# Token-major norms and gated output weights in a kernel with two interleaved batches

## The chip, the cores and the metric

The kernel runs on one core of a Trainium2 chip. The metric is device time in microseconds for one launch. Of the kernel before three runs are shown; their median counts.

## The reference, cut to what matters

Sixteen batches of 512 tokens with 128 channels pass through an adaptive layer: a norm with a scale and shift per batch, an attention with 16 heads, a gated addition to x, a second such norm, and a two-layer windowed transformer with a gated addition.

```python
mod = (_silu(c) @ wmod).reshape(16, 6, 1, -1)
sa, ca, ga, sb, cb, gb = (mod[:, i] for i in range(6))
ga, gb = ...                                # magnitude at least 0.25
h = _layernorm(x) * (1 + ca) + sa
x = x + ga * attn(h)                        # causal, 16 heads of 8, output @ W_O
h = _layernorm(x) * (1 + cb) + sb
x = x + gb * ffn(h)                         # 2 layers: windowed attention, norm, gated GELU
```

## The kernel before

All 16 batches are independent; batch b uses buffer set b % 2, and two batches are always in work: while one is in its attention (`max`, `score`, `ctx`, `turn`), the other is in the transformer (`qkv`, `rotate`, `wscore`, `wexp`, `share`, `pturn`, `wctx`, `wout`, `hid`, `down`). Every batch is one list of some 190 steps (`steps()`, line 55). A step is named, and each engine has its own code for it (`step` in each engine's function); the engines meet through semaphores, and PSUM banks are handed out in the order of a written table (`Banks.take`, line 202), whose waits stand on TensorE.

The order is written by hand tables. `PLACES` (line 91) is one order of the steps for all engines, `PARTS` says which engines take part, and `TURNS` (line 114) merges the two running batches on each engine. `merged` (line 136) joins them.

Activations lie channels in the partitions, tokens along the free dimension. The first norm (n = 0) goes so: `load` transposes x on TensorE (4 transposes of 128x128), ScalarE copies the result into `xT1` (line 664), GpSimd keeps a copy `xT` (line 1013); `center` multiplies with the centring matrix (line 444, one float32 product 512 wide, two instructions); ScalarE squares (676); `spread` multiplies with the averaging matrix (458); ScalarE takes Ln and Exp (685, 687); VectorE multiplies with the scale (865) into `y1`; the shift enters later as `added`, its products with the three weights, in lines 696, 875 and 731. From `y1` come queries, keys (470) and values (474). Their three bfloat16 parts are spread over partitions by DMAs (line 1080).

The attention ends with `join` (transposes, line 731), `out` (544: one product 512 wide) and line 912, which adds the gated result to `xT`. The second norm (n = 1) repeats `center`, `spread` and `scale` on `xT`; its result goes to `hs` (lines 994 and 790, half of the channels each, one of them moved by one token) and, on GpSimd, to `hT` (1035). The transformer's own norms (n = 2, 3) use the same steps. At the end `final` transposes `xT` back and VectorE copies it (989) for the store. The next x is loaded in step `load` (1096).

## Time and profile before

| | |
|---|---|
| median of 3 runs | 2214.65 us (2211.29 to 2220.58) |
| profiled execution: time, span | 2209.04 us, 2207.2 us |
| TensorE busy | 1993.5 us, 90% |
| ScalarE busy | 1592.4 us, 72% |
| VectorE busy | 1519.8 us, 69% |
| GpSimd busy | 842.4 us, 38% |

Busy time is the union of an engine's instructions; the extents of TensorE's instructions overlap, since they are pipelined, so the distance between starts says what one occupies. A wait is shown with what released it.

### The profile page before, as it was taken

What the parts mean: (1) busy time and instruction counts of PE and PEld (TensorE: products, weight loads), DVE (VectorE), ACT (ScalarE), POOL (GpSimd) and SP (SyncE); (2) the same over time, 40 slices, a digit from 0 to 9 for tenths busy, and PEclk for the clock granted to TensorE, in tenths of its full rate; (3) what the DMA queues carried; (4) which work ended last, traced back from release to release, by engine and by line L of the source; (5) the groups of instructions that cost most, each with busy time, mean ns of one, the idle gap of its engine ahead of it and who ended that gap; (6) DMA issues with size and microseconds to landing.
All of it is one profiled execution on the core that took longest, in us unless ns stands there. A gap on an engine that the chain in (4) does not pass through costs nothing. (4 is left out here: it accounts for less than half of the span.)

```text
span 2207.2 us, 55546 instructions
## 1 busy us (share of the span) xinstructions
PE 1993.5 (90%) x22104; PEld 1108.9 (50%) x22104; DVE 1519.8 (69%) x2383; ACT 1592.4 (72%) x3947; POOL 842.4 (38%) x778
## 2 busy tenths in 40 slices
PE   5689999899999989999999999999999999999966
PEld 3354545545454554545455454555545455554533
DVE  3485776767768676776867678686766867676743
ACT  1567858787786867768687786868678686867844
POOL 1142616245252623525163352515335162442531
PEclk7889999999999999999999999999999999999998
DMA  5110301302030130303103030310303012030000
GB/s 142 22 32 2 62 18 28 52 24 52 7 59 20 27 53 23 52 7 57 23 23 57 23 51 7 51 29 23 57 24 49 9 30 45 19 56 18 24 1 22
DMA packets 63106, 76.15 MB, mean 35 GB/s; under 512 B 10630, under 2 KB 57856, under 8 KB 60800
## 3 DMA queue, kind: packets, MB, share of 16 engines
q1 hardware_dynamic: 62852, 72.60, 18.2%
q8 instruction: 179, 2.93, 0.6%
q14 instruction: 75, 0.61, 0.1%
HBM read 9.14 MB, written 4.19 MB: 6 GB/s over the span
## 5 line engine op out<-in xcount | busy, mean ns | idle before, releaser
L1030 POOL TENSOR_TENSOR pr<-pr 128x1024 f32<-128x1024 f32 x128 | 302.1, 2360 | 665.8 <-DVE pr L934 665.3
L765 ACT ACTIVATE pr<-ps,wb,inv 128x128 f32<-128x128 f32 x768 | 339.2, 466 | 8.0 <-DVE wb L951 7.7
L888 DVE TENSOR_REDUCE nm<-ps 128x2 f32<-128x256 f32 (+2 forms) x384 | 310.7, 859 | 42.1 <-PE ps L412 41.5
L726 ACT ACTIVATE pr<-ps 128x1024 f32<-128x1024 f32 x320 | 311.4, 1030 | 31.6 <-PE ps L412 29.9
L1052 POOL TENSOR_TENSOR pr<-pr,shares 128x512 f32<-128x512 f32 x192 | 201.0, 1047 | 335.1 <-DVE shares L966 335.1
L393 PE MATMUL ps<-cf,pr 128*128 128x128 f32 x1792 | 262.6, 282 | 37.3 <-ACT scr L685 14.9
L393 PEld LDWEIGHTS ps<-cf,pr 128*128 128x128 f32 x1792 | 205.2, 144 | 147.7 <-issue 74.3
L927 DVE TENSOR_TENSOR pr<-ps,rot 128x1024 f32<-128x1024 f32 x128 | 156.7, 1224 | 143.0 <-ACT pr L738 117.6
L408 PE MATMUL ps<-cb 64*64 64x256 bf16 (+1 forms) x2560 | 177.6, 264 | 41.3 <-DMA keys<-early 18.2
L738 ACT ACTIVATE pr<-ps 128x1024 f32<-128x1024 f32 x128 | 131.3, 1026 | 88.7 <-PE ps L554 49.0
L959 DVE COPY pr<-ps 128x512 f32<-128x512 f32 x256 | 171.8, 677 | 18.3 <-PE ps L617 10.1
L945 DVE TENSOR_REDUCE wm<-ps 128x8 f32<-128x1024 f32 x128 | 155.5, 1215 | 26.3 <-PE ps L595 26.3
L408 PEld LDWEIGHTS ps<-cb 64*64 64x64 bf16 x2560 | 74.9, 105 | 186.0 <-issue 56.6
L765 ACT ACTIVATION_READ_ACCUMULATOR pr<-ps,wb,inv 128x1 f32 x768 | 164.3, 214 | 0.0
L934 DVE TENSOR_TENSOR pr<-ps,rot 128x512 f32<-128x512 f32 x256 | 163.6, 680 | 0.0
L526 PE MATMUL ps<-pr,V 128*16 128x512 f32 (+3 forms) x2048 | 151.7, 437 | 6.4 <-ACT pr L726 6.4
L936 DVE TENSOR_REDUCE scr<-pr 128x16 f32<-128x1024 f32 x128 | 154.6, 1208 | 0.0
L617 PE MATMUL ps<-pr 128*64 128x64 f32 x2048 | 132.5, 228 | 23.9 <-DVE pr L959 14.4
L617 PEld LDWEIGHTS ps<-pr 128*64 128x64 f32 x2048 | 106.6, 137 | 81.6 <-issue 35.8
L553 PE MATMUL ps<-Wqkv,hs 128*128 128x512 f32 x256 | 140.3, 631 | 6.6 <-ACT hs L790 3.0
L1045 POOL TENSOR_TENSOR pr<-pr,inv 128x512 f32<-128x512 f32 x128 | 133.4, 1042 | 19.6 <-POOL inv L1040 0.9
L595 PE MATMUL ps<-Kf,Q 64*64 64x128 f32 (+1 forms) x4096 | 139.8, 270 | 0.0
(158 smaller groups left out, 3988.3 us busy)
## 6 DMA issues: line engine op xcount, KB each, us to landing
pr<-V SPq DMA_DIRECT2D x32, 512.0 KB, 5.4
queries<-early SPq DMA_DIRECT2D x224, 64.0 KB
keys<-early SPq DMA_DIRECT2D x224, 64.0 KB
pr<-V SPq DMA_DIRECT2D x32, 384.0 KB, 6.9
xn<-in_L_attn_x SPq DMA_DIRECT2D x16, 256.0 KB, 2.8
out<-hT SPq DMA_DIRECT2D x16, 256.0 KB, 2.3
queries<-mT SPq DMA_DIRECT2D x128, 4.0 KB
Wqkv<-in_L_ffn_wqkv SPq DMA_DIRECT2D x1, 1536.0 KB
```

Source lines behind the costliest of these rows:

```text
L393: mm = pe.transpose(dst[:, t * P:(t + 1) * P], src(t), ident)
L408: pe.matmul(dst, identb[here, here], mask, start=True, stop=False, skip_group_check=True)
L617: mm = pe.matmul(bank[D2 * r:D2 * r + D2, q0:q0 + D2], val[s][:, t, 2 * p + r, :], PT[s][:, (2 * n + r) % 3, q0:q0 + D2], start=True, stop ...
L726: act.activation(dst, src, ACT.Exp, scale=SC1).then_inc(ex_r[s], 1)
L765: ins = act.activation(P2[s][2 * (p % 3) + r][:, o:o + P], bank[:, r * T + o:r * T + o + P], ACT.Exp, scale=inv[s][:, t, h:h + 1], bias=wb ...
L888: ins = dve.tensor_reduce(nm[s][:, qt, h:h + 2], src[:, :, o:o + (qt + 1) * P], AX_X, ALU.max, negate=True)
L927: dve.tensor_tensor(t1[s][i].rearrange("p (j h d) -> p j h d", j=2, h=H2), qk, cos, ALU.mult).then_inc(t_r[s], 1)
L934: dve.tensor_tensor(t2[s].rearrange("p (j h d) -> p j h d", j=2, h=H2)[:, :, :, o:o + 32], qk[:, :, :, q:q + 32], sin, ALU.mult).then_inc( ...
L945: dve.tensor_reduce(dst, src, AX_X, ALU.max, negate=True).then_inc(wm_r[s], 1)
L959: dve.tensor_copy(PT[s][:, (2 * n + r) % 3, :], bank).then_inc(pt_r[s], 1)
L1030: pool.tensor_tensor(t1[s][t % 3], t1[s][t % 3], t2[s], ALU.add).then_inc(sum_r[s], 1)
L1052: pool.tensor_tensor(part, part, share, ALU.mult).then_inc(part_r[s], 1)
```

## The change

Both outer norms are taken with tokens in the partitions. For x this is how it is loaded: `stats` runs `bn_stats` and `bn_aggr` on VectorE (four tiles of 128 tokens), ScalarE makes the inverse deviation from four variances per partition, and `plain` subtracts and multiplies, on GpSimd for norm 0 and on VectorE for norm 1. The result is transposed, and the scale and shift of the batch, now per partition, are applied while ScalarE and VectorE copy it from PSUM. The products of `center` and `spread` for n = 0 and 1, `xT`, `keep` and `added` are gone. The attention's output projection gives tokens in the partitions and adds to a buffer `x1`; its gate is put into the weights per batch (`gate`: GpSimd scales the transposed weights, TensorE transposes them back, ScalarE copies them). The final gate is a multiplication before the last transposes, and x1 is added after them. `PLACES` is now one list per engine instead of one for all; `TURNS` and the table of banks are new. The next x is loaded after line 912's successor.

```diff
-    out += [("turn", G1 - 1), ("join",), ("out",), ("center", 1), ("spread", 1), ("scale", 1)]
+    out += [("gate",), ("turn", G1 - 1), ("join",), ("out",), ("stats", 1), ("plain", 1), ("scale", 1)]
...
-PLACES = [
-    0, 1, 4, 2, 5, 10, 3, 6, 7, 8, 9, 11, 15, 12, 17, 14, 13, 18, 20, 16, 19, 22, 23, 28, 25, 29, 32, 30, 35, 31,
...
+PLACES = {
+    "PE": [
+        1, 2, 4, 6, 12, 10, 8, 11, 17, 16, 14, 19, 22, 20, 23, 25, 31, 40, 48, 21, 24, 38, 39, 26, 46, 45, 47,
...
+                    elif kind == "load":
                         bank, full = banks.take(pe, (b, "xT"), [xt_r.at(b, 1)])
+                        pe.wait_ge(*plain_r[0].at(b, 1))
+                        transposes(bank, lambda t: plain[:, t, :]).then_inc(full, 1)
+                    elif kind == "scale" and a[0] == 1:
+                        bank, full = banks.take(pe, (b, "yT"), [hsa_r.at(b, 1), hsp_r.at(b, 1), ym_r.at(b, 1)])
+                        pe.wait_ge(*plain_r[1].at(b, 1))
+                        transposes(bank, lambda t: y[s][:, t * P:(t + 1) * P]).then_inc(full, 1)
+                    elif kind == "gate":
+                        bank, full = banks.take(pe, (b, "gate"), [wg_r.at(b, 1)])
+                        pe.wait_ge(*wt_r.at(b, 1))
+                        pe.transpose(bank[:, 0:P], WoTg[:, :], ident).then_inc(full, 1)
...
-                        pe.matmul(bank, Wo1[:, :], y[s][:, :], start=True, stop=True).then_inc(full, 1)
+                        pe.wait_ge(*wg_r.at(b, 1))
+                        for t in range(NT):
+                            mm = pe.matmul(bank[:, t * P:(t + 1) * P], y[s][:, t * P:(t + 1) * P], Wog[s][:, :], start=True, stop=True)
+                        mm.then_inc(full, 1)
...
+                        act.wait_ge(*mv_r[n].at(b, 1))
+                        act.activation(dev[n][s][:, :], mv[n][s][:, :, 1], ACT.Ln, bias=eps[:, 0:1]).then_inc(dev_r[n][s], 1)
+                        act.wait_ge(*dev_r[n].at(b, 1))
+                        act.activation(dev[n][s][:, :], dev[n][s][:, :], ACT.Exp, scale=-0.5).then_inc(dev_r[n][s], 1)
...
+                        act.activation(y1, bank, ACT.Identity, scale=mod[:, 1, b:b + 1], bias=mod[:, 0, b:b + 1]).then_inc(xt_r[s], 1)
+                    elif kind == "scale" and a[0] == 1:
+                        bank = banks.wait(act, (b, "yT"))
+                        act.activation(hs[s][0:D2, :], bank[0:D2, :], ACT.Identity, scale=mod[0:D2, 4, b:b + 1],
+                                       bias=mod[0:D2, 3, b:b + 1]).then_inc(hsa_r[s], 1)
+                        act.wait_ge(*hsp_r.at(b, 1))
+                        if b >= S2:
+                            act.wait_ge(*stored.at(b, 0))
+                        act.activation(hT[s][:, :], bank, ACT.Identity, scale=mod[:, 4, b:b + 1],
+                                       bias=mod[:, 3, b:b + 1]).then_inc(ym_r[s], 1)
+                    elif kind == "gate":
+                        act.activation(Wog[s][:, :], banks.wait(act, (b, "gate"))[:, 0:P], ACT.Copy).then_inc(wg_r[s], 1)
...
+                        if i == 0 and b:
+                            act.wait_ge(*spread_r.at(b - 1, SPREADS))
+                        act.activation(parts[3 * i], bank, ACT.Copy).then_inc(hi_r[s], 1)
...
+                        for t in range(NT):
+                            dve.bn_stats(bn[n][s][:, t, :], (x1 if n else xn)[s][:, t, :]).then_inc(bn_r[n][s], 1)
+                        dve.wait_ge(*bn_r[n].at(b, NT))
+                        for t in range(NT):
+                            ins = dve.bn_aggr(mv[n][s][:, t, :], bn[n][s][:, t, :])
+                        ins.then_inc(mv_r[n][s], 1)
+                    elif kind == "plain" and a[0] == 1:
+                        dve.wait_ge(*dev_r[1].at(b, 2))
+                        for t in range(NT):
+                            ins = dve.tensor_scalar(y[s][:, t * P:(t + 1) * P], x1[s][:, t, :], mv[1][s][:, t, 0:1], dev[1][s][:, t:t + 1],
+                                                    ALU.subtract, ALU.mult)
+                        ins.then_inc(plain_r[1][s], 1)
...
+                        if n == 1:
+                            bank = banks.wait(dve, (b, "yT"))
+                            dve.tensor_scalar(hs[s][D2:P, 1:T], bank[D2:P, 0:T - 1], mod[D2:P, 4, b:b + 1], mod[D2:P, 3, b:b + 1],
+                                              ALU.mult, ALU.add).then_inc(hsp_r[s], 1)
...
-                        dve.scalar_tensor_tensor(xT[s][:, :], bank, mod[:, 2, b:b + 1], xT[s][:, :], ALU.mult,
-                                                 ALU.add).then_inc(x1_r[s], 1)
+                        dve.tensor_tensor(x1[s][:, :, :].rearrange("p t c -> p (t c)"), banks.wait(dve, (b, "out")),
+                                          xn[s][:, :, :].rearrange("p t c -> p (t c)"), ALU.add).then_inc(x1_r[s], 1)
...
+                    if kind == "plain" and a[0] == 0:
+                        pool.wait_ge(*dev_r[0].at(b, 2))
+                        if b:
+                            pool.wait_ge(*v1_r.at(b - 1, 1))
+                            pool.wait_ge(*hi_r.at(b - 1, 2))
+                        for t in range(NT):
+                            ins = pool.tensor_scalar(plain[:, t, :], xn[s][:, t, :], mv[0][s][:, t, 0:1], dev[0][s][:, t:t + 1],
+                                                     ALU.subtract, ALU.mult)
+                        ins.then_inc(plain_r[0][s], 1)
+                    elif kind == "gate":
+                        if b < S2:
+                            pool.wait_ge(prep_act, 10)
+                            pool.wait_ge(prep_dve, 11)
+                        if b:
+                            pool.wait_ge(*wg_r.at(b - 1, 1))
+                        pool.tensor_scalar(WoTg[:, :], WoT[:, :], mod[:, 2, b:b + 1], None, ALU.mult).then_inc(wt_r[s], 1)
...
-                    elif kind == "scale" and a[0] == 1:
-                        pool.wait_ge(*y_r[1].at(b, 1))
...
-                    elif kind == "load":
-                        banks.wait(sp, (b, "xT"))
+                    elif kind == "out":
+                        sp.wait_ge(*x1_r.at(b, 1))
```

Written out, the new order of TensorE from `out` of batch 1 on, with batch 0 in its second layer and batch 2 next (batch:step), is: 1:out, 0:wscore 2, 0:wscore 3, 0:pturn (0,0), 0:pturn (0,1), 1:scale 1, 2:load, 0:pturn (1,0), 0:wctx 0, 1:qkv 0. VectorE's is 1:out, 1:stats 1, 0:share (0,0), 0:share (0,1), 0:wscore 2, 0:share (1,0), 1:plain 1; GpSimd's 0:share (0,0), 0:share (0,1), 2:plain 0, 0:share (1,0). Before, TensorE had 1:out, 0:wscore 2, 1:center 1, 2:load, 0:pturn (0,0), 1:spread 1, 0:pturn (0,1), 0:pturn (1,0), 0:wscore 3, 1:qkv 0.

## Rows read from the trace of the kernel before

**Rows 1.** The page: busy time, instructions; TensorE's clock in 40 slices, tenths.

```profile
PE 1993.5 (90%) x22104; PEld 1108.9 (50%) x22104; DVE 1519.8 (69%) x2383; ACT 1592.4 (72%) x3947; POOL 842.4 (38%) x778
...
PEclk7889999999999999999999999999999999999998
```

**Rows 2.** Busy time by stretch: start:end, length, engines (instructions), clock, DMA share, GB/s.

```profile
480.00:1998.00 1518.00, 1419.72 (x16100) 792.41 (x16089) 1104.75 (x1726) 1158.19 (x2904) 616.32 (x564) 0.99 0.20 35
...
870.00:880.00 10.00, 7.72 (x96) 4.60 (x94) 7.03 (x14) 9.97 (x39) 5.19 (x5) 1.00 0.31 79
```

**Rows 3.** Line 912 alone: count, duration min/median/max in ns, first and last start.

```profile
L912 DVE SCALAR_TENSOR_TENSOR xT<-ps,mod,xT x16: 750/751/752, 101.3 to 2041.1; 128x512 f32<-128x512 f32 x16
```

**Rows 4.** TensorE's waits, 480 to 1998 us: total us, times, longest.

```profile
PE ps L393 <- ACT scr L685: 13.8, 12, 1.1
```

**Rows 5.** Timeline of TensorE: start, extent, what [idle before <-releaser].

```profile
787.11 1.05 PE L474 MATMUL ps<-Wv,early 128*128 128x128 f32 x8
...
870.03 1.12 PE L544 MATMUL ps<-y,Wo 128*128 128x512 f32 x2
...
871.09 0.41 PE L586 MATMUL ps<-cb 64*64 64x512 bf16 x4
...
872.30 1.12 PE L444 MATMUL ps<-xT,cf 128*128 128x512 f32 x2
...
873.26 0.60 PE L393 MATMUL ps<-cf,xn 128*128 128x128 f32 x4
...
873.70 0.60 PE L393 MATMUL ps<-cf,pr 128*128 128x128 f32 x4
...
876.45 0.65 PE L393 MATMUL ps<-cf,pr 128*128 128x128 f32 x4 [1.15 <-ACT scr L685]
...
878.87 0.41 PE L586 MATMUL ps<-cb 64*64 64x512 bf16 x4 [0.94 <-ACT pr L765]
...
880.13 1.10 PE L553 MATMUL ps<-Wqkv,hs 128*128 128x512 f32 x2
...
885.19 1.02 PE L444 MATMUL ps<-xturn,cf 128*128 128x512 f32 x2
...
886.05 0.60 PE L393 MATMUL ps<-cf,scr 128*128 128x128 f32 x4
```

**Rows 6.** Groups by line: busy us, mean ns of one | idle before.

```profile
L904 DVE TENSOR_TENSOR scr<-ps,rec 128x128 f32<-128x128 f32 x64 | 18.6, 291 | 2.2
...
L804 DVE CAST nmb<-nm 128x16 bf16<-128x16 f32 x64 | 11.2, 175 | 2.2
...
L1023 POOL TENSOR_SCALAR early<-rests 128x512 bf16<-128x512 f32 x32 | 19.8, 617 | 94.0 <-DVE rests L875 92.9
...
L1040 POOL TENSOR_SCALAR inv<-inv 128x16 f32<-128x16 f32 x128 | 34.5, 270 | 64.6 <-ACT inv L750 58.4
...
L748 ACT ACTIVATE scr<-scr 128x16 f32<-128x16 f32 x128 | 29.5, 231 | 21.9 <-DVE scr L936 21.9
...
L676 ACT ACTIVATE scr<-ps 128x512 f32<-128x512 f32 x48 | 28.8, 599 | 24.3 <-PE ps L444 24.3
...
L685 ACT ACTIVATE scr<-ps,eps 128x512 f32<-128x512 f32 x48 | 33.3, 694 | 29.5 <-PE ps L458 29.5
```

**Rows 7.** Timeline of the other engines in the same stretch.

```profile
871.20 0.75 DVE L912 SCALAR_TENSOR_TENSOR xT<-ps,mod,xT 128x512 f32<-128x512 f32 x1 [1.33 <-PE ps L544]
...
877.95 1.87 POOL L1035 TENSOR_SCALAR hT<-y,mod 128x512 f32<-128x512 f32 x1 [0.79 <-DVE y L865]
```

**Rows 8.** Timeline of the start: VectorE's line 825, then TensorE.

```profile
15.73 0.18 DVE L825 TENSOR_SCALAR mod<-mod 128x32 f32<-128x32 f32 x1
...
20.33 2.04 PE L470 MATMUL ps<-early,Wq 128*128 128x512 f32 x2 [1.22 <-DVE early L865]
...
46.33 0.43 PE L408 MATMUL ps<-cb 64*64 64x256 bf16 x4 [12.01 <-DMA keys<-early]
...
48.28 2.08 PE L458 MATMUL ps<-early,cf 128*128 128x512 f32 x2
```

More of the change, by code:

```diff
@@ L84, in steps @@
     return between + [(0, name) for name in out[:cut]]
-PLACES = [
[8 rows of a table removed]
-]
-PARTS = {
-    "PE": "center ctx down final hid join kheads load max out proj pturn qheads qkv rows1 score spread turn v values wctx wout wscore".split(),
-    "ACT": "center ctx down hid join kheads load norm proj qheads qkv rows1 scale score spread v values wctx wexp wout".split(),
-    "DVE": "center down final hid keep load max out proj pturn rotate scale share turn values wout wscore".split(),
-    "POOL": "keep norm proj rotate scale share values".split(),
-    "SP": "final load proj rows1 wscore".split(),
+PLACES = {
[8 rows of a table added]
+    "ACT": [
[6 rows of a table added]
+    "DVE": [
[5 rows of a table added]
+    "POOL": [
+        0, 3, 5, 7, 9, 15, 13, 18, 28, 30, 24, 35, 37, 42, 44, 50, 52, 32, 33, 70, 122, 127, 130, 133, 135, 137,
+        139, 145, 143, 148, 155, 157, 160, 162, 167, 169, 175, 177],
+    "SP": [
+        25, 31, 40, 48, 32, 33, 76, 82, 93, 106, 68, 158, 165, 173, 153, 125],
@@ L454, in step @@
+                        pe.wait_ge(*hsp_r.at(b, 2 * (n - 2) + 2))
+                        bank, full = banks.take(pe, (b, "xc", n), [sq_r.at(b, n - 1)])
+                        pe.matmul(bank, centre, hs[s][:, :], start=True, stop=True).then_inc(full, 1)
                     elif kind == "spread":
                         n, = a
[L456 to L457 removed]
@@ L508, in step @@
                             mm.then_inc(full, 1)
+                        if b == 0 and g == DEPTH:
+                            bank, full = banks.take(pe, "turned", [(prep_act, 10)])
+                            pe.wait_ge(ld_late, 16 * LATE)
+                            pe.transpose(bank[:, 0:P], Wo1[:, :], ident).then_inc(full, 1)
                     elif kind == "score":
```

306 lines of the change are left out of this document (132 added, 174 removed), and 24 rows, old and new, of the table PLACES.

## The prediction

> **What bounds the kernel now.** I read the page first, for shares and clock. TensorE is busy 90% of the span, ScalarE 72%, VectorE 69%, GpSimd 38%, and the granted clock sits at its upper level (2.4 GHz) except at both ends [rows 1]. The chain that ended last covers only the final 60 us, so it says nothing about the steady part. I therefore read the busy time by stage. Between 480 and 1998 us TensorE is busy 1419.7 of 1518 us, the others 1158 and 1105 [rows 2]. The reader should see the remainder: 98.3 us of idle TensorE. One batch takes 129.3 us (sixteen executions of line 912, the first at 101.3 and the last at 2041.1: 1939.8 / 15) [rows 3]. So the idle time is some 8.4 us per batch. The waits of TensorE in that stretch spread it over many small items; the largest, 13.8 us in 12 batches, is a transpose step that waits for ScalarE's line 685 [rows 4]. Line 685 is the logarithm of a norm.
>
> Then I looked at where in the batch that wait stands. The timeline around the end of the attention (t0 = 870.03, the start of the output projection, line 544) shows TensorE waiting 1.15 and 0.94 us within 9 us [rows 5]. From 870 to 880 us ScalarE is busy 9.97 of 10 us [rows 2]. So the kernel is bound by TensorE in most of the batch, and by ScalarE for 10 us or more after the attention. What the change does in that stretch decides how much of its gain arrives.
>
> **TensorE's own work.** Four float32 products 512 wide go for each batch: centre and spread of norm 0 and of norm 1. What one occupies is the distance to the next step's start, not its length: 872.30 to 873.26 is 0.96 us after a step of another kind, 885.19 to 886.05 is 0.86 us in a dense stretch [rows 5]. Two of each make 3.64 us. Added are four transposes of the second norm's result: 873.26 to 873.70, 0.44 us dense [rows 5], and 0.65 us where the step stands alone. I take 0.55. One more transpose, of the gated weights, is a quarter of that dense step at least (0.11) and 0.28 when alone; I take 0.2. The output projection becomes four products of 128 columns. Its nearest row is the step of line 474, whose eight instructions last 1.05 us at 787.11 where line 544 takes 1.12 us [rows 5]; I count nothing. The transposes of x remain, with another input. Net: 3.64 - 0.75 = 2.9 us less per batch, 46 us in sixteen.
>
> **ScalarE.** Squares, logarithms and exponentials 512 wide go: 0.60 us for the square and 0.69 for the logarithm (lines 676 and 685) [rows 6], and the exponential, SBUF to SBUF, between the two at 0.63; twice, 3.8 us. Added: four logarithms or exponentials of 4 columns, for which the nearest row is line 748 with 16 columns, 231 ns, 0.9 us together; one scaled copy of 512 columns into hT, 0.69 us as line 685; the copy of the gated weights, a quarter as wide, some 0.3. Net 1.9 us less. Of it, 1.9 - 0.5 - 0.7 = 0.7 us falls before the first `qkv` product of the batch.
>
> **VectorE.** Removed are two multiplications of line 865, 0.75 us each. Added are eight `bn_stats` and eight `bn_aggr`, which the trace doesn't have. Bounds for one: 175 ns (line 804, 16 elements) and 291 ns (line 904, 128 elements from PSUM) [rows 6]. I take 291 for `bn_stats`, which has line 904's size, and 175 for `bn_aggr`: 3.7 us per batch (2.8 to 4.7). Four subtractions and multiplications of 128 columns at 250 ns add 1.0. The second half of hs now comes from PSUM, 0.2 us more; the other replaced instructions differ by under 0.1 us each. Net +3.4 us per batch. VectorE has room on average (1105 + 41 of 1518 us), but not everywhere.
> The split into pieces of 128 columns is also what a rule warns of. The Trainium skill, "VectorE: DVE Perf Modes", section "The TRN2 errata", says that instructions reading SBUF pay a fixed latency each, and advises tiles of at least 512 elements. Its formula for a float32 add, (N + 151) / 0.96, gives 291 ns at 128 elements, which is what line 904 shows [rows 6]; four pieces would then cost 1.16 us where one of 512 costs 0.69 by that formula.
>
> **GpSimd.** Removed: the copy of x, as long as line 1023 (0.62 us) [rows 6], and the 512-wide addition of a per-partition scalar, line 1035, 1.87 us [rows 7]. Added: four operations of 128 columns with two per-partition scalars for the first norm, and one of 128 columns for the weights. Bounds for one: 0.15 us, a quarter of line 1023 with immediates (617 ns for 512), and 1.87 us, all of line 1035 [rows 6, 7]. I take a quarter of line 1035 and 0.08 of overhead, 0.55 us: 2.2 us for the four. In total GpSimd stays as busy as it was, but its place moves: the four stand between two `share` steps, whose results TensorE transposes next.
>
> **The order, walked through.** The new tables, written out as lists of steps, give TensorE after `out`: `wscore` 2 and 3, `pturn` (0,0), (0,1), the four transposes of norm 1, those of the next batch's x, `pturn` (1,0), `wctx` 0, then `qkv`. Times are from t0. The two `wscore` take 1.2 us each (871.09 to 872.30) [rows 5], so TensorE is free at 3.5. VectorE finishes x1 at 1.9 [rows 7], and has `stats` of norm 1 ahead of the first `share`: 1.9 + 1.9 + 0.2, and GpSimd's product (1.05) ends at 5.0. TensorE waits 1.5 us there and 0.6 at the second `pturn`. ScalarE reaches the two small functions at 5.1, VectorE the normalization at 5.9, ending at 6.9: a wait of 0.3. GpSimd ends the next batch's four operations at 8.3: a wait of 0.9, and its next `share` at 9.35: 0.6. `qkv` starts at 10.9, with one `wctx` (1.06) more done than before, where it started at 880.13, 10.1 after t0 [rows 5]. So 0.3 us is gained here: the old waits (1.15 + 0.94 us) are replaced by 3.9 us of new ones. The pair of norm 0 lay in a dense stretch and gives its whole 1.7 us, the weights' transpose takes 0.2. The walk gives 1.8 us per batch; if the new waits only equalled the old, it would be 2.9 or a little over. With upper bounds for unknown instructions in the walk, I take the middle, 2.4 us: 38 us in sixteen batches.
>
> **The start.** Batch 0 starts its projection at 20.33, having waited for line 865 behind two more products, Ln and Exp [rows 8]. With statistics taken directly from x, y1 needs only the modulation (line 825, written at 15.9) [rows 8] and the transposes; VectorE now handles both x tiles before it helps with the modulation, which costs it up to 2 us. I estimate y1 at 16.7, so 3.5 us earlier. TensorE then waits 12 us for the spread DMAs and does batch 1's spread, projections and values (5 us) between batch 0's maxima, from 48.28 on [rows 8]. The new order puts them into the 12 us: 2 us of that I count. The spread buffer is no longer needed for batch 1's norm, so no wait moves with it. The loads of x are issued after `out` instead of after the transposes; each has half a batch (60 us) of cover, and would cost some 2 us of landing if it had none. At the end nothing but the norm's latency changes: 0. Start: 5.5 us.
>
> **Sum.** 38 + 5.5 = 44 us off the profiled span of 2207.2 us (run 2209.04): 2163.7. The median of the runs shown, 2214.65, is 7.4 above that span; with that kept the forecast is 2171, rounded to 2170. The case's own range is 2150 to 2190 (0.8 us per batch of walk either way, and 4 at the start).
>
> **Rivals.**
> A. *The separate orders also close gaps.* 8.4 us per batch are idle; norm chains no longer hold TensorE's banks (line 685's 1.15 goes for certain), and engines no longer share one sequence. For it: the waits are spread over many steps. Against: the walk shows new ones. If all 2.9 us arrive and 1.4 more: 16 x 4.3 + 5.5 = 74, so 2140.
> B. *Half of it is absorbed.* In the stretch where ScalarE is full only its own 0.7 us counts and gaps return elsewhere: 1.0 us per batch, 16 + 4 = 20: 2195.
> C. *TensorE's busy figure is no bound.* Weight loads are busy 792 of 1518 us, 52% [rows 2]. If the array really waited on operands from the others, the removed products would leave idle time and nothing else, and the time would be 2214.65 less the start: 2209. Against: back-to-back products at 0.86 us leave no gap [rows 5]. The Trainium skill, "Perfetto Trace Analysis", section "Identifying the Most-Contended Engine", says that matmul busy share is no good measure and that weight-load share should be used; by that rule TensorE has ample headroom.
> D. *Slower: GpSimd's small operations hold back the shares.* They stand ahead of `share` (1,0) and of the transposes of x. Each us over my 2.2 is a wait of TensorE. Above 0.55 + 2.4 / 4 = 1.15 us an instruction the gain per batch is gone. At 1.87 us, if the price of line 1035 is one per instruction and not per column, it is 4 x 1.32 = 5.3 us more: 16 x (5.3 - 2.4) - 5.5 = 41 slower, 2256. For it: line 1035 costs three times line 1023 for no shown reason [rows 6, 7]. Against: such a fixed part doesn't appear in line 1040, 16 columns in 270 ns [rows 6].
> That the change doesn't do what it says is not open: the products are gone from the code.
>
> **How the numbers follow.** Forecast 0.50, A 0.20, B 0.12, C 0.10, D 0.08. About 0.5% (11 us) is what a measurement of this kernel can tell from no change. Forecast, A and B are faster: 0.82; C is the same: 0.10; D slower: 0.08. The range 2122 to 2206 takes in the forecast, B, most of A and part of C; it leaves out about 0.05 below and 0.13 above.
>
> **What would show it.** In the new profile: TensorE's busy time near 1993 - 46 = 1947 us and a period near 126.9; the wait for line 685 gone from a `pturn`; new waits of a `pturn` for GpSimd and of x's transposes for GpSimd's plain step; `bn_stats` between 175 and 291 ns; GpSimd's new instruction near 0.55 us. The first projection starts near 16.7. I am wrong if the period fell by less than 1 us although TensorE's work did, or if GpSimd's instruction is over 1.15 us.

## The result, and the profile after

The changed kernel takes 2196.5 us (median of 4, 2195.0 to 2197.7), the kernel before beside it 2213.3 (2211.3 to 2220.6). The ratio is 0.9918, 95% interval 0.9894 to 0.9942: 0.8% less, which is clear of the noise, but 17 us and not 44. The profiled execution of the changed kernel has a span of 2195.0 us against 2207.2.

The page of the changed kernel, busy time and TensorE's clock:

```profile
PE 1980.0 (90%) x22147; PEld 1136.5 (52%) x22147; DVE 1567.6 (71%) x2671; ACT 1613.8 (74%) x3975; POOL 864.6 (39%) x826
PEclk7889999999999999999999999999999999999897
```

TensorE was to fall from 1993 to 1947 us and is at 1980 [rows 1]. The page's row of tenths can't show why; the busy time by stretch does (start:end, length, PE, PEld, DVE, ACT, POOL, clock, DMA share, GB/s). The first row is the steady part, the others lie in one batch, around the end of its attention:

```profile
480.00:1998.00 1518.00, 1416.09 (x16117) 810.15 (x16116) 1140.52 (x1925) 1175.66 (x2895) 628.66 (x596) 0.97 0.17 34
864.00:869.00 5.00, 2.75 (x45) 1.85 (x38) 4.93 (x18) 4.97 (x23) 3.90 (x5) 0.98 0.01 4
869.00:876.00 7.00, 6.40 (x46) 4.59 (x47) 4.28 (x7) 4.16 (x15) 4.57 (x5) 0.52 0.01 2
876.00:880.00 4.00, 4.00 (x14) 1.88 (x13) 2.55 (x5) 3.93 (x14) 1.05 (x1) 1.00 0.01 2
```

Before, the first row read 1419.7 busy at a clock of 0.99 [rows 2]; now 1416.1 at 0.97. The work is less, and part of it runs at half rate: from 869 to 876 us the granted clock is 0.52, that is 1.2 GHz nearly throughout. I call such a stretch low. The same one, 6.8 us long, stands at the same place in each of the steady batches. In the kernel before, thirteen steady batches have five low stretches together, four of them of 3.4 us.

TensorE's timeline of that place (861.33, line 565, is the output projection; 874.58, line 575, the first `qkv` product):

```profile
861.33 1.16 PE L565 MATMUL ps<-Wog,y 128*128 128x128 f32 x8
866.30 0.63 PE L411 MATMUL ps<-cf,pr 128*128 128x128 f32 x4 [0.81 <-POOL pr L1089]
867.30 0.63 PE L411 MATMUL ps<-cf,pr 128*128 128x128 f32 x4 [0.38 <-POOL pr L1089]
868.93 1.12 PE L411 MATMUL ps<-cf,y 128*128 128x128 f32 x4 [1.00 <-DVE pr L995]
870.64 1.09 PE L411 MATMUL ps<-cf,early 128*128 128x128 f32 x4 [0.60 <-ACT y L796]
871.66 1.09 PE L411 MATMUL ps<-cf,pr 128*128 128x128 f32 x4
874.58 1.65 PE L575 MATMUL ps<-Wqkv,hs 128*128 128x512 f32 x2
```

Four waits, 2.8 us, within 5 us (I forecast five, 3.9 us), and from the third on the same set of four transposes ("a set" below) takes 1.09 to 1.12 us instead of 0.63. This answers to [rows 5]: line 685's wait [rows 4] is gone, as forecast, and the step it held up is 866.30 here. VectorE and GpSimd beside it:

```profile
863.67 0.87 DVE L845 BATCH_NORM_STATS2 scr<-x 128x6 f32<-128x128 f32 x4
864.58 0.38 DVE L848 BATCH_NORM_AGGREGATE mv<-scr 128x2 f32<-128x6 f32 x4
864.88 0.21 DVE L1002 RECIPROCAL shares<-sums 128x4 f32<-128x4 f32 x2
866.24 0.94 DVE L987 TENSOR_TENSOR wb<-wm,inv 128x8 f32<-128x8 f32 x1
867.19 1.08 DVE L853 TENSOR_SCALAR y<-x,mv,dev 128x128 f32<-128x128 f32 x4
868.19 1.28 DVE L995 COPY pr<-ps 128x512 f32<-128x512 f32 x2
...
865.10 2.05 POOL L1089 TENSOR_TENSOR pr<-pr,shares 128x512 f32<-128x512 f32 x2 [8.84 <-DVE shares L1002]
867.15 3.35 POOL L1046 TENSOR_SCALAR early<-xn,mv,dev 128x128 f32<-128x128 f32 x4
```

GpSimd works from 865.10 to 871.5 without a gap, so the wait put down to ScalarE at 870.64 was one for line 1046, which ends at 870.50. And 1.00 at 868.93 isn't for the norm (line 853 ends at 868.27) but for a PSUM bank: by the table of banks the transposed norm goes into the bank that the first `pturn` filled, which line 995 empties only behind the norm. (The filled kernel below confirms it: there a constant set that needs nothing but this bank waits 1.06 us.)

The lines of the new instructions (busy us, mean ns of one):

```profile
L1046 POOL TENSOR_SCALAR early<-xn,mv,dev 128x128 f32<-128x128 f32 x64 | 53.3, 842 | 6.7 <-ACT dev L693 6.7
L845 DVE BATCH_NORM_STATS2 scr<-x 128x6 f32<-128x128 f32 x64 | 14.0, 281 | 1.9 <-DVE x L948 0.5
L848 DVE BATCH_NORM_AGGREGATE mv<-scr 128x2 f32<-128x6 f32 x64 | 6.1, 158 | 0.5
L853 DVE TENSOR_SCALAR y<-x,mv,dev 128x128 f32<-128x128 f32 x64 | 18.1, 359 | 0.6 <-ACT dev L693 0.6
```

The start, TensorE's timeline; then line 948, the successor of line 912 [rows 3], in all sixteen batches (durations, first and last start) and in batch 2:

```profile
16.35 2.05 PE L485 MATMUL ps<-early,Wq 128*128 128x512 f32 x2 [0.96 <-ACT early L703]
43.11 0.43 PE L426 MATMUL ps<-cb 64*64 64x256 bf16 x4 [3.62 <-DMA keys<-early]
...
L948 DVE TENSOR_TENSOR x<-ps,xn x16: 682/684/692, 98.8 to 2030.2; 128x512 f32<-128x512 f32 x16
343.84 0.68 DVE L948 TENSOR_TENSOR x<-ps,xn 128x512 f32<-128x512 f32 x1
```

And the kernel before in batch 2:

```profile
353.46 0.75 DVE L912 SCALAR_TENSOR_TENSOR xT<-ps,mod,xT 128x512 f32<-128x512 f32 x1 [1.32 <-PE ps L544]
```

So the 12.2 us of span come as 9.6 by batch 2 (353.46 - 343.84), 1.2 over the thirteen batches after that, and 1.4 behind the last. (Start and end together were to give 5.5.) The steady part gained 0.1 us per batch where I had put 2.4.

To see where, I cut each steady batch at two events of TensorE's timeline: the output projection, and the first `qkv` product behind it. All kernels below are measured so (means of the 11 or 12 batches whose projection starts between 480 and 1985 us; the period is the mean distance between their projections, the rest the difference; the times are medians with the ratio to the kernel before on the same chip, whose medians were 2209.6 to 2213.3).

| kernel | time, us | ratio (95%) | out to `qkv` | rest | period |
|---|---|---|---|---|---|
| before | 2213.3 | | 10.52 | 119.29 | 129.81 |
| forecast | 2170 | | 10.9 | 116.6 | 126.9 |
| after | 2196.5 | 0.9918 (0.9894 to 0.9942) | 13.29 | 116.43 | 129.72 |
| after, filled | 2172.1 | 0.9842 (0.9820 to 0.9864) | 12.01 | 116.25 | 128.26 |
| after, shares first | 2182.4 | 0.9854 (0.9836 to 0.9872) | 12.19 | 116.30 | 128.49 |
| after, shares first, clock held | 2157.1 | 0.9751 (0.9716 to 0.9785) | 10.88 | 116.25 | 127.13 |

The rest of the batch shrank by 2.86 us, more than forecast. The stretch grew by 2.8 instead of 0.8. The kernel before isn't uniform, though: its five batches with a low stretch have 11.0 to 11.1 us from out to `qkv`, the other seven 10.10, and four of these have a period of 128.76 to 128.78. Against these four the changed kernel's steady batch is longer, not shorter. (In the forecast's row the rest is 129.3 - 10.1 less 2.56 for the pair, the gate and the moved `wctx`; that is the walk, 127.5 together. The period of 126.9 is what I took.)

### The profile page after: what moved, and what is told of

Read it like the earlier page. It is cut to its first block, busy times and chain, and to the rows that moved or that the text cites. A ratio compares the mean times of both kernels' runs of the same rounds, so it can differ in the third digit from the quotient of the medians.

```text
span 2195.0 us, 55933 instructions
## 1 busy us (share of the span) xinstructions
PE 1980.0 (90%) x22147; PEld 1136.5 (52%) x22147; DVE 1567.6 (71%) x2671; ACT 1613.8 (74%) x3975; POOL 864.6 (39%) x826
## 4 chain that ended last, share of the span: by engine, by line
PE 71%; ACT 14%; DVE 7%; issue 4%; SPq 2%; DMA 1%; POOL 1%; DVEq 0%; ACTq 0%; POOLq 0%
PE ps L411 13%; PE ps L639 7%; PE ps L545 7%; ACT pr L796 6%; PE ps L575 6%; PE ps L648 5%; PE ps L585 5%; PE ps L430 4%; PE ps L576 4%; PE ps L668 4%; PE ps L426 3%; PE ps L617 3%; PE ps L659 3%; PE ps L662 2%; DVE wm L981 2%
## 5 line engine op out<-in xcount | busy, mean ns | idle before, releaser
L411 PE MATMUL ps<-cf,pr 128*128 128x128 f32 x1792 | 268.1, 287 | 51.8 <-POOL pr L1089 29.9
L426 PE MATMUL ps<-cb 64*64 64x256 bf16 (+1 forms) x2560 | 176.6, 266 | 24.5 <-DVE nm L928 12.9
L796 ACT ACTIVATION_READ_ACCUMULATOR pr<-ps,wb,inv 128x1 f32 x768 | 174.5, 227 | 0.0
L802 ACT ACTIVATE scr<-ps 128x512 f32<-128x512 f32 x128 | 76.1, 623 | 117.5 <-PE ps L639 117.5
L575 PE MATMUL ps<-Wqkv,hs 128*128 128x512 f32 x256 | 148.5, 664 | 7.9 <-ACT mT L740 3.1
L639 PE MATMUL ps<-pr 128*64 128x64 f32 x2048 | 145.6, 241 | 8.3 <-DVE pr L995 5.6
L639 PEld LDWEIGHTS ps<-pr 128*64 128x64 f32 x2048 | 113.5, 149 | 62.7 <-issue 42.9
```

The lines of the kernel that those rows point to most:

```text
L411: mm = pe.transpose(dst[:, t * P:(t + 1) * P], src(t), ident)
L426: pe.matmul(dst, identb[here, here], mask, start=True, stop=False, skip_group_check=True)
L575: pe.matmul(bank[:, 0:T], lhs, Wqkv[:, l, 0:T], start=True, stop=True)
L639: mm = pe.matmul(bank[D2 * r:D2 * r + D2, q0:q0 + D2], val[s][:, t, 2 * p + r, :], PT[s][:, (2 * n + r) % 3, q0:q0 + D2], start=True, stop ...
L796: ins = act.activation(P2[s][2 * (p % 3) + r][:, o:o + P], bank[:, r * T + o:r * T + o + P], ACT.Exp, scale=inv[s][:, t, h:h + 1], bias=wb ...
```

## The experiments

Two theories. **Clock**: the four waits bring TensorE down to 1.2 GHz, and half rate eats the work saved. **Order**: the new chain through VectorE and GpSimd holds TensorE up, whatever its clock. Then there is the prediction's rival C: TensorE's work was no bound, so removing it brings nothing.

### Filling the waits of the changed kernel

```diff
 # pturn of the second layer's first pair, after the bank is taken
+if l == DEPTH - 1 and p == 0:
+    transposes(bank, lambda t: ident)
 # scale 1, after the bank: two sets; load, for b >= 2: one set
+transposes(bank, lambda t: ident)
```

> The changed kernel, with extra transposes of a constant on TensorE ahead of four of its waits after the attention (one set of four before each of the two first pturn steps of layer 1 and before the transposes of the next x, two sets before the transposes of the second norm). Nothing waits less; the idle time is only filled, and the extra work is 5 x 0.46 = 2.3 us per batch. Theory 1 (the granted clock falls to its lower level for 6.8 us in every batch because TensorE is idle so often just before, and that gives the saved work back): the low stretches go, the period falls from 129.7 to some 126.7 to 127.5, the time to about 2150 to 2165 us. Theory 2 (the new waits themselves take the gain, the clock only follows): the time stays at 2197 or rises by up to 10 us, even if the clock stays up.

2172.1 us: 24 us less with 2.3 us more work per batch. No low stretch is left in the steady batches. The time lies between the two ranges: the clock theory had the right sign and asked for at least 7 us more. The busy row and the timeline (`cf` alone marks a constant set):

```profile
480.00:1998.00 1518.00, 1428.69 (x16510) 820.22 (x16512) 1152.11 (x1940) 1191.33 (x2921) 637.40 (x602) 1.00 0.17 34
861.97 0.66 PE L411 MATMUL ps<-cf,pr 128*128 128x128 f32 x4 [0.62 <-POOL pr L1095]
864.70 1.09 PE L411 MATMUL ps<-cf 128*128 128x128 f32 x8 [1.06 <-DVE pr L1001]
866.50 0.60 PE L411 MATMUL ps<-cf,early 128*128 128x128 f32 x4
867.43 0.63 PE L411 MATMUL ps<-cf,pr 128*128 128x128 f32 x4 [0.34 <-POOL pr L1095]
869.07 1.12 PE L579 MATMUL ps<-Wqkv,hs 128*128 128x512 f32 x2
```

Worked out: busy per batch here is 1428.69 / 1518 x 128.26 = 120.7, less 2.3 filled is 118.4, against 121.4 before: the 3.0 us of work really went (2.9 forecast). In the changed kernel 121.0 are shown, so half rate cost 2.6 us of busy time. Of that, 1.3 us reached the stretch (13.29 to 12.01); the rest had lain beside waits. The Trainium skill, "TensorE: Matmul & The Clock Gate", section "HAM oscillation — how this bites in real kernels", describes a loop whose wait drops the clock in every iteration. The changed kernel's trace agrees in that it falls once in every batch, 129.7 us from one fall to the next; but the page's loop has one wait for a transfer, of some 3 to 5 us, and here it is four waits of 0.38 to 1.00 us. The same page says under "Part 4: PE-mode transpose" that transposes don't engage the full clock; here transposes against an identity, as filling, kept it at 2.4 GHz (granted clock 1.00 where it was 0.97), so the measurement decides.

Is a filled set itself on the path? One set less ahead of the second norm:

> The first fill with one set instead of two ahead of the second norm's transposes (1.85 us of filled work instead of 2.3). If each filled set there lies on the path, 0.4 us per batch is gained while the clock holds: 2163 to 2170. If the clock then falls again in some batches, it goes back towards the changed kernel: 2172 to 2192. If the stretch is set by the other engines once the clock holds, nothing changes: 2170 to 2174.

2170.8 us (ratio 0.9824, 0.9802 to 0.9847), stretch 11.99, no low clock. The third case: with the clock held, other engines set this stretch at 12.0, and it isn't 10.9. In the timeline above the last wait, 0.34 us, is for GpSimd's third share.

Only the two sets of the `pturn` pair:

> The changed kernel with only the two sets at the first pturn pair filled in (0.9 us of work). If the waits just before the fall (0.81 and 0.38 us) decide, the clock stays at 2.4 GHz and the stretch from out to qkv is under 12: 2165 to 2176. If the wait for the second norm (1.00 us) is enough by itself, the low stretch stays, perhaps shorter: 2180 to 2197.

2184.6 us (0.9889, 0.9868 to 0.9911): the second case. Low stretches of 3.4 us remain in 11 of 13 batches; out to `qkv` 11.96 in the two without one among the eleven measured, 12.9 to 13.5 in the others. The later waits count too.

And the same filling in the kernel before:

> The kernel before with the same 2.2 us of constant transposes per batch: two sets ahead of spread 1's product, one at each of the first pturn pair, one ahead of x's transposes. If the filled kernels gain by holding the clock, there is little of it here (few stretches at 1.2 GHz in the steady part), and what lies on TensorE's path is added: out to qkv 10.5 to 11.6, 2208 to 2228. If filling is a gain of its own, whatever the clock (an earlier start of what follows), it gives 20 us here too: about 2190.

2220.4 us (1.0045, 1.0030 to 1.0060), out to `qkv` 11.34. Filling is no gain of its own; it pays where the clock was falling. Here the sets lie partly on TensorE's path: 11.34 against the 10.10 of the unfilled batches without a low stretch.

### A wait added to the kernel before

```diff
+if l == DEPTH - 1 and p == 0:
...
+pool.tensor_scalar(P2[s][r], P2[s][r], 1.0, 0.0, ALU.mult, ALU.add).then_inc(slow, 1)
+pool.wait_ge(slow, len(slowed))
```

> The kernel before, with a 0.62 us in-place copy on GpSimd ahead of each of the first two share steps of layer 1, so that TensorE's first pturn steps after the attention wait up to 1.2 us longer. Theory 1: the added idle time lets the clock fall in every batch, and the time rises by more than the wait itself, 3 to 5 us per batch: 2260 to 2290 us. Theory 2: at most the added wait, 0.6 to 1.2 us per batch: 2223 to 2232 us, with the clock near 0.975.

2207.3 us (0.9990, 0.9972 to 1.0008), out to `qkv` 10.43: nothing. A miss for both theories as I had put them (2260 to 2290, 2223 to 2232), and the timeline says why: TensorE's wait of 1.15 us for line 685 [rows 4] covered the delay. It now waits 0.16 for GpSimd and 0.94 for the same logarithm, 1.1 as before. I had counted GpSimd's delay and not TensorE's idle time, so the run tells nothing of the clock.

### Work removed from the kernel before, and then with the clock held

```diff
 # the four products of norms 0 and 1 alone
+left, right = (a.bitcast(BF16).rearrange("p (n x) -> p n x", x=2)[:, :, 1] for a in (left, right))
 return pe.matmul(bank, left, right, start=True, stop=True)
```

> The kernel before, with the four products of norms 0 and 1 done from the upper halves of the float32 numbers, as bfloat16: 512 columns in one short product instead of a float32 one; the results are only approximate. TensorE does some 2.6 us less per batch and nothing else moves. If TensorE's work is what bounds (both theories on the change assume it) 30 to 42 us come off: 2172 to 2183 us. If the shorter products bring out new low-clock stretches, as theory 1 holds for the change, it is less, and the records show the low stretches in more batches than before. If TensorE's busy time were no bound, 2213.

2213.3 us (1.0009, 0.9994 to 1.0025). 2.6 us of TensorE's work are out and not one microsecond arrives. Its busy row, its longest wait and the first `qkv` behind it:

```profile
480.00:1998.00 1518.00, 1406.19 (x15922) 785.70 (x15944) 1100.20 (x1716) 1152.26 (x2885) 615.95 (x563) 0.98 0.20 34
874.20 1.97 PE L393 MATMUL ps<-cf,pr 128*128 128x128 f32 x8 [1.86 <-ACT scr L690]
878.89 1.99 PE L558 MATMUL ps<-Wqkv,hs 128*128 128x512 f32 x2
```

The wait that was 1.15 us [rows 5] is 1.86: TensorE only arrives earlier at ScalarE's logarithm. After it, the products run at half rate (1.99 us for two instead of 1.10 [rows 5]), now in all 13 steady batches (six of the low stretches are 3.4 us long, seven 6.8). Two readings are possible: the clock took the gain, or there was none (rival C). They part when the clock is held:

> The kernel before with norm 0's and 1's products thinned to bf16 (approximate results, 2.6 us less work per batch) and the same constant transposes filled in as in the filled kernel before (2220.4). Beside that run it tells what the removed work is worth with the clock held. If only the clock took the gain of the thinned kernel, all 2.6 us arrive: about 2180. If two of the four products lie in a stretch that ScalarE bounds and two in a dense one, half: 2195 to 2205. If removed products leave idle time and nothing else: 2215 to 2222.

2198.8 us (0.9951, 0.9936 to 0.9966). The second case. Beside the filled kernel before (2220.4) the same thinning is now worth 22 us, 1.4 per batch: 1.1 in the stretch, 0.3 in the rest. The steady rows, first of the filled kernel before, then of the one thinned as well:

```profile
480.00:1998.00 1518.00, 1426.56 (x16261) 810.21 (x16259) 1097.37 (x1717) 1149.49 (x2896) 616.39 (x564) 1.00 0.20 35
```

```profile
480.00:1998.00 1518.00, 1419.10 (x16370) 803.92 (x16387) 1111.81 (x1739) 1161.32 (x2913) 616.38 (x564) 1.00 0.20 35
```

So in the filled kernel about half of these products' time counts, and the clock is up in both. That is less than it seems, because the filling itself had lengthened TensorE's path (11.34 in the stretch), and 1.1 of the 1.4 us come off there: the kernel thinned and filled has 10.21 and a commonest period of 128.71 us, the kernel before, in its four batches without a low stretch that take 128.8, has 10.10 and 128.77. What thinning alone would be worth there at 2.4 GHz no run shows, since the kernel that is only thinned fell in every batch: the fall and ScalarE's wait (1.86 us) both hide it.

### The same in the changed kernel

The products of norms 2 and 3 are thinned in the same way, with the filling and without:

> The changed kernel with constant transposes filled in, as in the run that kept the clock, and with the four products of norms 2 and 3 read as bf16 from the upper halves (approximate results, 2.6 us less TensorE work per batch, in the dense part). If TensorE's work bounds the dense part as soon as the clock holds, the period falls from 128.2 to 125.6 to 126.4: 2131 to 2145. If products removed only leave idle time, it stays near 2172 (2166 to 2178). If the new idle time lets the clock fall there, stretches at 1.2 GHz come back at the thinned products and less than half of the 2.6 us arrives: 2152 to 2172.

2174.5 us (0.9824, 0.9794 to 0.9854), where the filled kernel took 2172.1. By its time this is the second case (2166 to 2178), by its trace the third, and more strongly: low stretches came back in ten of 13 batches, in another place (clock 0.50 from 936 to 940 us, 76 us behind x1), next to a thinned product. Of the eleven measured batches the three without one took 127.4 to 127.8 us (128.2 in the filled kernel), those with one of 6.8 us 129.7 to 129.9. So even at 2.4 GHz only 0.4 to 0.8 of the 2.6 us arrived; the rest left idle time, as rival C says. A wait for a transfer stands just ahead of the low stretch (933.11 us, 1.86) that was short before, 4.0 us in 12 batches. It is now:

```profile
PE ps L430 <- DMA queries<-mT: 22.3, 12, 1.9
```

That is 1.5 us more per batch, which is where most of the removed work went.

> The changed kernel with the same thinned products of norms 2 and 3 and nothing filled in. If work removed arrives whatever the clock does, 16 x 2.6 = 42 us: about 2155. If the clock takes it back as in the kernel before with thinned products, the gain is under 15 us: 2182 to 2200, with stretches at 1.2 GHz longer than 6.8 us or two in each batch.

2187.3 us (0.9875, 0.9854 to 0.9895), 9 us of 42: the second case. Out to `qkv` 13.09, rest 115.93, and five of the batches have a second low stretch, 77 us behind the projection.

### Order: who sets the stretch at 12.0

GpSimd's normalization of the next x, ahead of the shares in its own order:

```diff
-        0, 3, 5, 7, 9, 15, 13, 18, 28, 30, 24, 35, 37, 42, 44, 50, 52, 32, 33, 70, 122, 127, 130, 133, 135, 137,
+        0, 3, 5, 7, 9, 15, 13, 18, 24, 28, 30, 35, 37, 42, 44, 50, 52, 32, 33, 70, 122, 127, 130, 133, 135, 137,
```

> The changed kernel with one place changed in GpSimd's order: its four operations on the next x stand before the first two share steps of the other batch, where GpSimd is idle, and no longer between them and the third. Theory 2 (GpSimd's 3.35 us hold back the third share and the transposes of x): the waits of TensorE for these (0.60 and what follows) shrink, period about 128.5, time 2175 to 2185. Theory 1 (the clock): the first three waits (0.81, 0.38, 1.00 us) stay, so unless the low stretch goes too, the time stays within 5 us of 2197.

2185.7 us (0.9898, 0.9872 to 0.9924), 0.7 us above the second theory's range; stretch 12.53 (10.9 to 13.4, with a low stretch of 3.4 or 6.8 us in ten of the eleven measured batches). The one without a low stretch tells most:

```profile
1762.68 1.16 PE L565 MATMUL ps<-Wog,y 128*128 128x128 f32 x8
1771.02 0.65 PE L411 MATMUL ps<-cf,y 128*128 128x128 f32 x4 [1.73 <-DVE pr L995]
1773.59 1.10 PE L575 MATMUL ps<-Wqkv,hs 128*128 128x512 f32 x2
```

It has 10.91 from out to `qkv`, though TensorE waits as long as before (1.30, 0.38 and 1.73 us), because nothing waits behind the second norm's transposes. So with the clock up and GpSimd's step out of the way the stretch isn't 12.0 but 10.9. Then the same work on VectorE:

> The changed kernel with one thing moved: the four small normalizations of the next batch's x run on VectorE, in the gap before the attention's end, instead of on GpSimd between two share steps. If GpSimd's 3.35 us there is a cause of the missing gain, TensorE's waits of 0.60 us (transposes of x) and those for the next share go, fewer or shorter stretches at 1.2 GHz follow, and the period falls from 129.7 to 128.0 to 128.6: 2169 to 2180. If only the waits at the first pturn pair (0.81 and 0.38) and at the second norm (1.00) decide the clock, the low stretch stays and 8 us come at most: 2188 to 2196. If VectorE's 1.1 us ahead of the score maxima holds up the exponentials, the time is 2197 to 2207.

2196.4 us (0.9925, 0.9910 to 0.9941): no gain, the upper end of the second case. The wait of x's transposes went, and two ahead of it grew; first TensorE's rows, then VectorE's:

```profile
865.75 0.63 PE L411 MATMUL ps<-cf,pr 128*128 128x128 f32 x4 [1.29 <-POOL pr L1095]
869.36 1.11 PE L411 MATMUL ps<-cf,y 128*128 128x128 f32 x4 [1.97 <-DVE pr L1008]
...
866.84 1.86 DVE L863 TENSOR_SCALAR y<-x,mv,dev 128x128 f32<-128x128 f32 x4
868.62 1.27 DVE L1008 COPY pr<-ps 128x512 f32<-128x512 f32 x2
```

VectorE's normalization took 1.86 us instead of 1.08, while GpSimd multiplied from 866.80 to 867.85. The clock fell in each batch as before, out to `qkv` 13.34. How much of this is the clock's and how much VectorE's this run can't tell; in the batch above VectorE's chain is nearly as late (1.73 us of wait, not 1.97), and at 2.4 GHz it has 10.91.

VectorE's statistics behind the first two reciprocals:

```diff
+for b in range(1, B):
+    at = ORDER["DVE"].index((b, ("stats", 1)))
...
+    ORDER["DVE"].insert(at + 2, ORDER["DVE"].pop(at))
```

> The changed kernel with VectorE taking the two reciprocals of the first share pair before the statistics of the second norm (1.3 us) and not behind them. If the waits around the attention's end are what replaced the gain, the first wait (0.81 us) goes and with it 0.5 to 1.2 us per batch, half of the low clock included: 2177 to 2188. If it only moves the wait to the second norm's transposes (1.00 us becomes up to 2), the time stays at 2193 to 2199.

2182.4 us (0.9854, 0.9836 to 0.9872), the first case: 14 us for a swap that removes no work: GpSimd's normalization starts 1.0 us earlier behind x1 (3.26 us, not 4.27), the stretch is 12.19, and the low stretches are mostly 3.4 us long. Then swap and filling together, with three sets ahead of the second norm:

> The changed kernel with the first two reciprocals ahead of the second norm's statistics, and five sets of constant transposes (2.2 us of work): two in the first pturn pair, three ahead of the second norm's transposes, where the shares-first run waited 2.34 us. If clock and order are two separate losses (they gave 25 and 14 us alone), the stretch from out to qkv falls under 11.5 us (12.0 and 12.2 alone) and the time is 2150 to 2166. If both remove the same loss, the low clock, it stays at 2168 to 2180.

2193.7 us (0.9924, 0.9907 to 0.9940), out to `qkv` 13.48: outside both ranges, 14 us above the upper one. The timeline shows the fault:

```profile
868.18 2.68 PE L415 MATMUL ps<-cf 128*128 128x128 f32 x12 [2.39 <-DVE pr L1003]
870.66 1.06 PE L415 MATMUL ps<-cf,y 128*128 128x128 f32 x4
```

The three sets stand behind the wait for the bank, not in it: 2.39 us idle and then 2.5 us of filling at a falling clock. The same with GpSimd's step on VectorE:

> As the run with both the fill and the shares first, and the next batch's normalization on VectorE instead of GpSimd. If GpSimd's 3.3 us are the next limit of the stretch once the clock is held, x's transposes and the third share come up to 0.9 us earlier: 6 to 14 us less than without the move, 2140 to 2158. If VectorE is the limit (its second-norm step took 1.86 us beside GpSimd's share in the run with the move, 1.08 us without), the move costs: 2160 to 2175.

2217.5 us (1.0027, 1.0012 to 1.0042), a stretch of 14.7 or 15.8 us in turn: again outside both ranges, and 24 us above the kernel without the move. TensorE's wait for the bank is 3.14 us where it was 2.39, behind a normalization that took VectorE 1.81 us and not 1.15, and the three sets still follow it.

With the pair's sets alone, and then with one more ahead of x's transposes:

> Shares first, with constant transposes (0.9 us) only in the first pturn pair, none ahead of the second norm. In the run with both, TensorE waited 2.4 us for the bank of the second norm's transposes and then did the three filled sets on its path; if that was the reason for 2193.7, this kernel loses the 1.3 us per batch again and comes to 2165 to 2182 (between, if one short stretch at 1.2 GHz stays). If it was the low clock that the 2.4 us wait brings in any case, it stays at 2182 or above.

> As the run with shares first and the pair filled, plus one constant set ahead of the transposes of x (0.44 us more). If the clock needs work up to there, 2160 to 2175 and fewer stretches at 1.2 GHz than without it; if that set only lies on the path, up to 7 us slower than without it.

2164.3 (0.9798, 0.9775 to 0.9822) and 2164.7 us (0.9797, 0.9773 to 0.9820): as good as each other, with six low stretches each from 480 us on. So the misplaced sets were the reason for 2193.7, and the set ahead of x's transposes neither helps nor costs. The first is the cleanest measure of the clock, since its batches come in two kinds, 127.05 and 128.2 us long. One of the second kind (the first two rows) beside one of the first (the last two):

```profile
730.80:733.80 3.00, 1.41 (x10) 1.21 (x11) 2.77 (x6) 3.00 (x14) 2.54 (x3) 0.97 0.01 3
733.80:736.80 3.00, 3.00 (x37) 2.54 (x36) 2.24 (x5) 1.36 (x3) 1.32 (x2) 0.50 0.02 5
859.00:862.00 3.00, 1.39 (x11) 1.19 (x12) 2.79 (x7) 3.00 (x14) 2.56 (x3) 1.00 0.00 0
862.00:865.00 3.00, 3.00 (x40) 1.92 (x38) 2.57 (x5) 2.54 (x8) 1.65 (x2) 1.00 0.00 0
```

Same idle time ahead (1.4 of 3 us busy), same work behind, clock 0.50 or 1.00; out to `qkv` 11.8 to 12.1 or 10.86. A low stretch of 3.4 us costs 0.9 to 1.3, mostly 1.2 us. If so, a filling that lies in the bank's wait and holds the clock in every batch should bring all to 127.05:

```diff
+for _ in range(4 if r else 1):
+    transposes(bank, lambda t: ident)
```

> Shares first, with the first pturn of the pair filled by one set and the second by four (2.2 us of constant work), which lies in the 2.38 us for which TensorE otherwise waits for VectorE's copy (that copy stands behind the second norm in VectorE's order, so a later pturn costs nothing). In the run with the pair filled alone, batches with a 3.4 us stretch at 1.2 GHz took 128.2 and those without 127.05. If that difference is the clock's, all batches now take 127.05: 0.55 us per batch less, 2150 to 2160. If the difference has another cause, the two lengths stay: 2162 to 2168.

2157.1 us (2155.1 to 2157.8; 0.9751, 0.9716 to 0.9785). All measured periods but one (127.4) are 127.1, out to `qkv` 10.88, and this beats both kernels, by 39 us the changed one.

```profile
480.00:1998.00 1518.00, 1437.67 (x16753) 829.67 (x16752) 1150.38 (x1958) 1200.61 (x2949) 639.62 (x605) 1.00 0.17 35
852.84 1.91 PE L415 MATMUL ps<-cf 128*128 128x128 f32 x16
856.27 0.66 PE L415 MATMUL ps<-cf,y 128*128 128x128 f32 x4 [1.08 <-DVE pr L1002]
859.18 1.13 PE L579 MATMUL ps<-Wqkv,hs 128*128 128x512 f32 x2
```

Of all these kernels it has the busiest TensorE, and it is the fastest.

## Why the prediction was right and wrong

**TensorE's work** (-2.9 us per batch): right, 3.0 by the filled kernel. The rest of the batch gave 2.86 where the steps put there make 2.56; 0.6 of the 2.86 is that the kernel before's mean includes its irregular batches.

**The walk of the order** (out to `qkv` 10.9, took 2.4 us per batch): this step failed. The stretch is 13.25 in nearly every batch. The step from the walk's own 1.8 to 2.4 had no ground either: it appealed to upper bounds for unknown instructions, and GpSimd's 0.55 us stood in the walk between bounds of 0.15 and 1.87. The sum of the walk's errors:

- *The clock*, 1.3 us. Every step of the walk was priced at 2.4 GHz. I listed 3.9 us of waits within 5 us and took them for idle time alone; they also bring the next 6.8 us to 1.2 GHz. Shown: filled, the stretch is 12.0; in the shares-first kernel with the pair filled the two kinds of batch differ by 1.2.
- *GpSimd's price*, 0.9 to 1.0 us. One instruction is 842 ns, not 550: 3.35 us for the four, not 2.2. It ended 9.2 us after the output projection's start, not 8.3, and the third `share` at 10.2, not 9.35; with the transposes and the `wctx` behind it that makes 12.0, which the filled kernel has. Two things removed it: GpSimd's step placed earlier (10.91, but in one batch only) and VectorE's order, which lets the same step start 1.0 us sooner (10.88 in all of them). Both needed the clock up; with the step on VectorE and the clock falling nothing was gained.
- *The bank*: I had 0.3 for the second norm's transposes, it was 1.00, since the bank hangs on a copy behind the norm. It lay beside GpSimd's 3.35 us, so it moved only the clock.
- *The base*: I took 10.1 from one batch; the mean of the kernel before is 10.52, and its steady period 129.81, since [rows 3] average in a short first period. This is 0.4 in the change's favour. It is the clock again: the five batches with a low stretch have 11.0 to 11.1. The prediction has the clock at its upper level except at both ends [rows 1]; the tenths hide these five. The trace could have shown before the change what a fall costs here, 1.0 us.

10.1 to 10.9 was 0.8 of loss; + 1.3 + 1.0 - 0.4 gives 2.7, measured 2.8. Against 2.86 gained in the rest that leaves 0.1.

**The start** (5.5 us): what the forecast named came about. The first projection is at 16.35 (16.7 forecast), and TensorE's wait for the transfers fell from 12.01 [rows 8] to 3.62. But the 9.6 us by batch 2 don't follow from it. Line 948 starts 2.5 us before line 912 in batch 0 (98.8 and 101.3), 2.5 us behind it in batch 1 (214.2 and 211.7), and 9.6 us before it in batch 2; and in the first 98 us TensorE is busy 61.3 us where it was 61.9, so its idle time only moved. By the end of batch 0 the start is worth 2.5 us. Between batches 1 and 2 lie 12.1 us (141.8 before, 129.7 now), as much as the whole difference of the spans. What gives them stays open; the forecast has nothing there.

**VectorE's prices**: `bn_stats` 281 ns (291 taken), `bn_aggr` 158 (175). But a run of four takes 0.87 us and 0.38, less than four means, since they overlap in part; so the pieces of 128 didn't cost what the formula for one makes of them (1.16 us). The normalization is 359 ns (250 taken), four of them 1.08 us.

**The rivals.** A expected the idle time to shrink too; the stretch took new waits, as the walk said. B gave the right time (2195) by another mechanism, which is luck: in the stretch the engines beside TensorE and its clock took the gain, elsewhere nothing came back. C as put is refuted by the rest of the batch, where 2.2 to 2.9 us came off for the 2.56 of the steps; but thinned products elsewhere brought nothing with the clock falling, and 0.4 to 0.8 of 2.6 us with it up, so in part C holds for them. Only beside 2.2 us of filling were they worth half. D's mechanism was there, at 0.84 us and under its point of 1.15. The row "TensorE's busy time near 1947" told it: 1980, with the removed work gone, is slower work.

**Left open.** Three kernels with a low stretch in each batch (after, the move to VectorE, the first combined fill) have a mean period of 129.7 although their work differs, and the batches with 6.8 us of it in the filled and thinned one come to 129.7 to 129.9. It is no rule: shares first (128.5), the thinned kernel before (130.4) and the combined fill with the move (131.4) fall in each batch too. Why the four meet I didn't test. Nor was the second norm given another bank: its neighbours are all in use at that point.

## What to carry to other kernels

When a change takes work from a busy TensorE and leaves waits close together, price the steps behind these waits at 1.2 GHz as well, and look up the granted clock around them, batch by batch, already in the trace before: the shares of the whole span hide it. A removed product is worth its time only where nothing else ends last and the clock stays; and filling that lies on TensorE's path makes a later removal look worth more than it is. Test a suspected clock by filling constant work into the waits, ahead of operands but not behind a wait for the bank; and before paying for it, look whether an engine's order alone closes the wait (here two reciprocals ahead of 1.3 us of statistics: 14 us).

## What the runs showed of the hardware

- A clock held by filling made the kernel faster with more TensorE work: 2.2 us of constant transposes per batch, 25 us less in the shares-first kernel (2182.4 to 2157.1).
- GpSimd's `tensor_scalar` with two per-partition scalars took 842 ns for 128 columns; with one, line 1055, 615 ns, while 512 columns with immediates are 617 ns [rows 6]. Its price is neither per column nor per instruction alone.
- VectorE's two-input operation on 8 elements (line 987) took 0.17 us alone and 0.94 beside GpSimd's product, ending with it (867.18 and 867.15); its float32 `tensor_scalar` 1.08 and 1.86. The Trainium skill, "GPSIMD Engine Reference", section "1. Specifications", states that the two engines share SBUF interfaces and that VectorE's operations with two SBUF inputs, or in a two-port mode, contend there; the trace agrees for the operation with two inputs, and in which mode the `tensor_scalar` ran no run shows.
